# Penalties of one key tile: a product on VectorE in place of two matmuls on TensorE, last batch of a decoder layer

## The reference

```python
penalties = res * scope                          # 512 x 512 for a batch, one for all heads
log_pen = jnp.log(jnp.maximum(penalties, 1e-32))
scores = jnp.einsum('bhqd,bhkd->bhqk', q, k) / np.sqrt(HEAD_DIM)
scores = scores + log_pen[:, None, :, :]
probs = jax.nn.softmax(scores, axis=-1)
ctx = jnp.einsum('bhqk,bhkd->bhqd', probs, v)
x = _layernorm(x + ctx.transpose(0, 2, 1, 3).reshape(b, s, h))
```

## Time and profile before

| | us |
|---|---|
| median of 3 runs | 752.32 |
| the profiled execution | 752.63 |
| its span | 750.8 |
| TensorE busy (matmul) | 662.1 (88%) |
| VectorE busy | 593.8 (79%) |
| ScalarE busy | 475.9 (63%) |
| GpSimd busy | 324.7 (43%) |
| L1585, low half of the logarithm, 128 matmuls | 49.2 |
| L748, GpSimd's products, 128 | 167.3 |
| L1037, row maxima of self groups, 256 | 168.1 |

### The profile page before, as it was taken

How to read it: one execution, slowest core, us unless ns; L and a number is a source line. 1 busy time by engine, 2 the same in 40 slices (tenths; PEclk the granted TensorE clock), 3 DMA queues, 4 the chain that set the end, 5 groups by cost and what they waited for, 6 DMA issues and landing times.

```text
span 750.8 us, 10494 instructions
## 1 busy us (share of the span) xinstructions
PE 662.1 (88%) x3398; PEld 267.2 (36%) x3402; DVE 593.8 (79%) x1290; ACT 475.9 (63%) x795; POOL 324.7 (43%) x418
## 2 busy tenths in 40 slices
PE   6468989999899989999799999898898899987973
PEld 3233324443233243344232433342223235233441
DVE  3997988687898986678997867568997796836997
ACT  3515756646558868655469688454677776792965
POOL 6305868555665414646464126546722200101404
PEclk9678999989999999999999999999999999999997
DMA  2722352300322314312203403431511420000003
GB/s 92 205 62 85 109 149 95 105 8 21 108 74 83 92 46 115 87 46 73 71 26 87 109 24 87 109 91 24 157 48 43 130 68 22 3 4 1 1 1 112
DMA packets 35926, 53.98 MB, mean 72 GB/s; under 512 B 5281, under 2 KB 26913, under 8 KB 35873
## 3 DMA queue, kind: packets, MB, share of 16 engines
q1 hardware_dynamic: 35872, 53.31, 25.7%
HBM read 37.04 MB, written 14.68 MB: 69 GB/s over the span
## 4 chain that ended last, share of the span: by engine, by line
PE 52%; DVE 26%; POOL 8%; ACT 6%; issue 6%; DMA 2%; SPq 0%; POOLq 0%; DVEq 0%; ACTq 0%
PE ps L1604 11%; PE ps L1557 9%; PE ps L1580 9%; PE ps L1441 6%; DVE dist L1040 5%; PE ps L1544 5%; POOL probs L748 5%; ACT probs L933 4%; PE ps L1537 3%; DVE mx L1037 3%; PE ps L1584 2%; PE ps L1585 2%; DVE pen_a L1107 1%; DVE x L1077 1%; DVE stats L1062 1%
## 5 line engine op out<-in xcount | busy, mean ns | idle before, releaser
L1557 PE MATMUL ps<-KS,QS 96*128 96x512 bf16 x512 | 200.2, 394 | 37.8 <-DVE mx L1037 16.5
L933 ACT ACTIVATE probs<-ps 128x512 f32<-128x512 f32 x256 | 149.5, 596 | 120.5 <-PE ps L1580 66.1
L748 POOL TENSOR_TENSOR probs<-probs,penT 128x512 f32<-128x512 f32 x128 | 167.3, 1327 | 110.0 <-ACT probs L933 109.9
L1580 PE MATMUL ps<-QS,KS 108*128 108x512 bf16 x512 | 195.8, 384 | 10.7 <-ACT probs L933 5.6
L933 ACT ACTIVATE probs<-ps,mask_col 128x512 f32<-128x512 f32 x256 | 166.9, 688 | 45.7 <-PE ps L1580 43.4
L1037 DVE TENSOR_REDUCE mx<-ps 128x1 f32<-128x512 f32 x256 | 168.1, 682 | 34.7 <-PE ps L1557 34.1
L1040 DVE CUSTOM_DVE_ANT_0 dist<-ps,mask_rest 128x512 bf16<-128x512 f32 x192 | 125.7, 684 | 21.3 <-PE ps L1557 21.0
L1557 PEld LDWEIGHTS ps<-KS,QS 96*128 96x128 bf16 x512 | 50.7, 99 | 176.1 <-DVE mx L1040 61.9
L1580 PEld LDWEIGHTS ps<-QS,KS 108*128 108x128 bf16 x512 | 50.0, 98 | 87.9 <-ACT probs L933 49.5
L1604 PE MATMUL ps<-probs,v_s 128*32 128x512 f32 x512 | 69.1, 611 | 2.7 <-POOL probs L748 2.7
L1604 PE MATMUL ps<-probs,v_c 128*32 128x512 f32 x512 | 68.2, 604 | 0.9 <-ACT probs L933 0.9
(11 more groups left out here) (195 smaller groups left out, 937.0 us busy)
## 6 DMA issues: line engine op xcount, KB each, us to landing
parts_qs<-parts SPq DMA_DIRECT2D x8, 384.0 KB, 2.4
parts_ks<-parts SPq DMA_DIRECT2D x8, 384.0 KB, 2.8
KS<-parts_ks SPq DMA_DIRECT2D x16, 192.0 KB, 3.4
QS<-parts_qs SPq DMA_DIRECT2D x16, 192.0 KB, 3.8
parts_kc<-parts SPq DMA_DIRECT2D x8, 384.0 KB, 2.8
KS<-parts_kc SPq DMA_DIRECT2D x16, 192.0 KB, 2.9
parts_qc<-parts SPq DMA_DIRECT2D x8, 384.0 KB, 2.9
QS<-parts_qc SPq DMA_DIRECT2D x16, 192.0 KB, 3.4
```

What stands on the lines that cost most here:

```text
L748: g.tensor_tensor(probs[:, T % NP, :], probs[:, T % NP, :], penT[:, MUL_KT.index(kt), :], ALU.mult)\
L933: s_.activation(probs[:, T % NP, :], ps[:, exp_bank(T), :], ACT.Exp, bias=bias)\
L1557: mm(ps[:, MAX_BANKS[(TG * n + i) % AHEAD], :], QS[0:SK, slot, j, t * P:(t + 1) * P], KS[0:SK, slot, j, :], start=True, stop=True).then_in ...
L1580: ins = mm(o, KS[0:SM, slot, j, kt * P:(kt + 1) * P], QS[0:SM, slot, j, :], start=True, stop=not logged)
```

## The change

A key tile (`VEC_KT` = 1) of the self groups from batch `VEC_FROM` = 3 on, which is the last batch, gets its penalties by a product on VectorE after the exponential. Its penalties are prepared as `penT` (a third plane), not as logarithm halves. TensorE issues one matmul in place of three for these 16 tiles, and `context` of that key tile waits for VectorE's products and is issued a slot later. VectorE's job "penalise" is in the slot of the exponential and runs three slots late, behind that slot's row maximum and ahead of the other late jobs. The functions `by_vector`, `by_vector_until` and `kept` are new; `logs` counts only the tiles that still have a logarithm.

```diff
--- before.py
+++ after.py
@@ -44,9 +44,10 @@
 SILUS = 4
 RING = 4
 MUL_KT = (0, 2)
+VEC_KT, VEC_FROM = 1, 3
 
 DVE_LAG, ACT_LAG, POOL_LAG = 2, 0, 1
-DVE_LATE = {"norm": 3, "v": 3, "wo": 3, "lpB": 3}
+DVE_LATE = {"norm": 3, "v": 3, "wo": 3, "lpB": 3, "penalise": 3}
 ACT_LATE = {"middle": 3}
 POOL_LATE = {"low": 5, "shift": 0}
 NP = 8
@@ -72,6 +73,11 @@
 def place(what, part):
 
     return PARTS - 1 - part if what == "k" else part
+
+
+def by_vector(b, kt):
+
+    return b >= VEC_FROM and kt == VEC_KT
 
 
 class Step:
@@ -154,6 +160,10 @@
             at = [(0, ("shift", s.shift)), (3, ("m", s.shift))] + list(at)
         if s.p2 is not None:
             at = [(10, ("last_context", s.p2)), (10, ("oT", s.p2)), (15, ("norm", s.p2))] + list(at)
+        for slot in range(TG):
+            e = s.exp_at(slot)
+            if e and groups[e[0]][0] == "s" and by_vector(groups[e[0]][1], e[1] // GH):
+                s.items[slot].append(("penalise", *e))
         for slot, job in at:
             s.items[slot].append(job)
         for lo, hi, task in tasks:
@@ -338,7 +348,7 @@
         lp = sb("lp", [P, NT, S], F32, att)
         lpT_hi = sb("lpT_hi", [P, NT - len(MUL_KT), S], F16, att)
         lpT_lo = sb("lpT_lo", [P, NT - len(MUL_KT), S], F16, att)
-        penT = sb("penT", [P, len(MUL_KT), S], F32, att)
+        penT = sb("penT", [P, len(MUL_KT) + 1, S], F32, att)
         V = {w: sb("v_" + w, [P, NT, NH, VC], F32, att) for w in "sc"}
         probs = sb("probs", [P, NP, S], F32, att)
         mx = sb("mx", [P, 2, NT, GH], F32, att)
@@ -391,6 +401,7 @@
         rest_made = sem("rest_made")
         middle_made = sem("middle_parts_made")
         pen_applied = sem("penalties_applied")
+        pen_by_vector = sem("penalties_applied_by_vector")
         gate_ready = sem("gate_weights_ready")
         max_scores = sem("scores_for_max")
         max_done = sem("max_done")
@@ -482,7 +493,15 @@
 
         def logs(b, kt):
 
-            return len(log_kt) * b + log_kt.index(kt) + 1
+            return [(i, k) for i in range(b + 1) for k in log_kt if not by_vector(i, k)].index((b, kt)) + 1
+
+        def by_vector_until(n):
+
+            return GH * sum(kind == "s" and by_vector(b, VEC_KT) for kind, b, _ in groups[:n + 1])
+
+        def kept(b, kt):
+
+            return MUL_KT.index(kt) if kt in MUL_KT else len(MUL_KT)
 
         def multiplied(n, kt):
 
@@ -882,10 +901,12 @@
 
                         if kt in MUL_KT:
                             act.wait_ge(pen_applied, multiplied(last_self(b - 1), kt))
-                        else:
+                        elif by_vector(b - 1, kt):
+                            act.wait_ge(pen_by_vector, by_vector_until(last_self(b - 1)))
+                        elif not by_vector(b, kt):
                             act.wait_ge(exp_scores, TG * last_self(b - 1) + GH * (kt + 1))
-                    if kt in MUL_KT:
-                        s_.activation(penT[:, MUL_KT.index(kt), :], bank(u), ACT.Copy, scale=2.0 ** LN_SHIFT)\
+                    if kt in MUL_KT or by_vector(b, kt):
+                        s_.activation(penT[:, kept(b, kt), :], bank(u), ACT.Copy, scale=2.0 ** LN_SHIFT)\
                             .then_inc(side_free[u % 2], 1)
                     else:
                         s_.activation(lpT_hi[:, log_kt.index(kt), :], bank(u), ACT.Copy).then_inc(lp_hi_made, 1)
@@ -1092,7 +1113,7 @@
                     if b:
 
                         dve.wait_ge(lp_made, b)
-                        used(dve, *[unit[("lpB", b - 1, kt)] for kt in MUL_KT])
+                        used(dve, *[unit[("lpB", b - 1, kt)] for kt in range(NT) if kt in MUL_KT or by_vector(b - 1, kt)])
                 if k == 0:
                     leave(v.tensor_scalar(pen_a[:, :], z_row[:, :], -1.0, wi, ALU.mult, ALU.add))
                 elif k == 1:
@@ -1176,6 +1197,15 @@
                     penalty(*job[1:])
                 elif what == "norm":
                     normalise(job[1])
+                elif what == "penalise":
+                    n, i = job[1:]
+                    T, b = TG * n + i, groups[n][1]
+                    if groups[n][2] == 0 and i % GH == 0:
+
+                        used(dve, unit[("lpB", b, VEC_KT)])
+                    dve.wait_ge(exp_done, T + 1)
+                    v.tensor_tensor(probs[:, T % NP, :], probs[:, T % NP, :], penT[:, len(MUL_KT), :], ALU.mult)\
+                        .then_inc(pen_by_vector, 1)
                 elif what == "v":
                     w, b, i = job[1:]
                     full(dve, u)
@@ -1463,7 +1493,7 @@
                         ins.then_inc(side_full[u % 2], 1)
                 elif what == "lpB":
                     b, kt = job[1:]
-                    src = pen if kt in MUL_KT else lp
+                    src = pen if kt in MUL_KT or by_vector(b, kt) else lp
                     pe.wait_ge(pen_made if kt in MUL_KT else lp_made, b + 1)
                     turn(u, [src[:, t, kt * P:(kt + 1) * P] for t in range(NT)])
                 elif what == "x1T":
@@ -1566,7 +1596,7 @@
                     pe.wait_ge(shift_loaded, 16 * (n + 1))
                     if n < RING:
                         pe.wait_ge(own_rows_made, n + 1)
-                logged = kind == "s" and kt not in MUL_KT
+                logged = kind == "s" and kt not in MUL_KT and not by_vector(b, kt)
                 if logged and g == 0 and j == 0:
 
                     used(pe, unit[("lpB", b, kt)])
@@ -1598,6 +1628,8 @@
                 T = TG * n + GH * kt
                 if kind == "s" and kt in MUL_KT:
                     pe.wait_ge(pen_applied, multiplied(n, kt))
+                elif kind == "s" and by_vector(b, kt):
+                    pe.wait_ge(pen_by_vector, by_vector_until(n))
                 else:
                     pe.wait_ge(exp_done, T + GH)
                 for j in range(GH):
@@ -1621,7 +1653,8 @@
                     if e:
                         exp_tile(*e)
                         kt = e[1] // GH - 1
-                        by_product = groups[e[0]][0] == "s" and kt in MUL_KT
+                        kind, b, _ = groups[e[0]]
+                        by_product = kind == "s" and (kt in MUL_KT or by_vector(b, kt))
                         if kt >= 0 and e[1] % GH == (GH - 1 if by_product else GH - 2):
                             context(e[0], kt)
                     for job in s.items[i]:
```

## The result

The changed kernel took 760.16 us in the median (758.12 to 761.29, four runs), the kernel before 751.7 beside it: a ratio of 1.0095, 95% interval 1.0062 to 1.0128. The forecast was 755.3 in a range of 748.0 to 760.5. So it is slower, by 7 to 8 us where the sum said 3.0. It lies inside the range by 0.3 us, in the part that was left open for the rivals; the forecast's own range ended at 758.3. The rival that gave 760.3, the clock, was the nearest.

What follows compares the result with a forecast made beforehand. TensorE held 52% of the chain, VectorE 26%; VectorE was the fuller engine in groups three and four. Terms 0.7 - 0.9 + 1.8 + 1.8 - 0.4 = +3.0 us gave 755.3 us against the median, range 748.0 to 760.5.

Steps and rivals of the forecast that it cites:

- the forecast's own range: 753.3 to 758.3 us, for VectorE's queue and the meetings taking TensorE's gain and more, +1 to +6 us; chance 0.54.
- the clock: Rival: longer TensorE idling before 513.66 and 535.66 brings a second 1.2 GHz stretch, plus more meetings; +8 us, 760.3; chance 0.15.
- Removed: 32 matmuls off TensorE in the last batch's four self groups, 7.0 us, taken as the bound on any gain there.
- Preparation: One tile turned from pen, VectorE's low-half subtraction of 0.69 us dropped where VectorE idles anyway; taken as 0.
- First group: To the mark at 476.21: no TensorE gain, two meetings delay GpSimd; +0.7 us, bounds 0 and +1.5.
- meetings: VectorE's two-SBUF-input products and GpSimd instructions holding each other up: up to 1.1 us for VectorE, 0.4 for GpSimd each.
- Second group: TensorE's slot 3 comes 1.9 us sooner, a context product of 1.0 us moves behind it; -0.9 us, bounds -1.7 and +0.4.
- Third group: VectorE's queue from 512.92 to 527.30 takes four products, less 0.64 us idle; +1.8 us, bounds +0.7 and +3.5.
- Fourth group: Slot 3's maximum comes 3.0 us later, less 1.2 lead, and the moved context product adds 1.0; +1.8 us, bounds +0.3 and +3.
- Give-back: At 555.65, where VectorE waits 1.40 us for TensorE, part of the delay is returned; -0.4 us, bounds 0 and -1.4.
- Faster: Rival: TensorE's gain in slots 12 to 15 holds where TensorE is the bound; -5.0 us, 747.3; chance 0.21.
- Nothing: Rival: the delays are absorbed by 555 us and the first two group terms cancel; 752.5 us; chance 0.10.

Runs made afterwards that it cites:

- e3: Changed kernel without VectorE's products or any wait for them, key tile 1's penalties left out in the last batch: 754.78 us, ratio 1.0027.
- e9: Changed kernel with ten filler matmuls into a free bank ahead of TensorE's wait for GpSimd in the first group: 759.68 us, ratio 1.0104.
- e12: The changed kernel run once more without any edit, for its trace: 757.88 us, a single execution.
- e1: Changed kernel with the normalisation ahead of VectorE's product in slot 15, nothing else: 756.36 us, ratio 1.0061.
- e2: Changed kernel with VectorE's 16 products replaced by memsets of the same tile, those penalties left out in the last batch: 756.67 us, ratio 1.0067.
- e7: Key tile 3 in place of 1, its logarithm matmuls removed, no products, its penalties left out: 750.18 us, ratio 0.9960 against the kernel before.
- e6: Changed kernel with key tile 3 in place of 1 given to VectorE: 759.22 us, ratio 1.0083.
- e8: Kernel before the change with eight filler matmuls ahead of its third wait, the 2.73 us at 513.66: 752.74 us, ratio 1.0006.
- e4: Changed kernel with two filler score matmuls put back ahead of each of the 16 exponential tiles, products kept: 756.35 us, ratio 1.0066.
- e5: Changed kernel with both the normalisation ahead of VectorE's product in slot 15 and two filler matmuls a slot: 759.61 us, ratio 1.0086.
- e11: Changed kernel without products, those penalties left out, and with two filler matmuls in each of the 16 slots: 752.82 us, ratio 1.0002.

## Why the prediction was right or wrong

**Removed, 7.0 us: the size was right, the use was not.** It was taken as a bound, and the waits behind it took all of it, as e3 shows (1.0027 with nothing in their place).

**Preparation, 0.** Between the marks of 439.27 and 457.89 after and before differ by 0.01 us. Right.

**First group, +0.7.** The meetings were right. GpSimd's instructions at 466.71 and 468.28 took 1.61 and 1.71 us where unmet ones took 1.16 and 1.27: 0.45 a meeting, 0.4 predicted. By the Trainium skill (SBUF — State Buffer, Who interferes with whom) the two exclude each other for the whole instruction, which by the 0.61 us of an unmet product would be 0.6, an estimate; the trace has GpSimd lose less, and VectorE 0.54 at 466.09. Nine of the sixteen products took over 1 us, where a third was expected. e9 gives +0.82 for the step with the wait filled. What failed is the sentence that the wait would be about 2 us and cost no more than its length: it was 3.11, and in after's trace 1.40 us of lower clock came behind it.

**Second group, -0.9: the term that failed most.** The prediction followed VectorE to the maximum that slot 3 asks for, and took the normalisation as one piece of that queue. It did not ask who waits for the normalisation: TensorE, for the side bank, ahead of slot 3. That wait of 2.33 us and the clock behind it make +2.9 (+2.7 in e12). With the normalisation ahead (e1) +0.3 is left, and without meetings (e2) 0.0; the full -0.9 appears only without the products (e3).

**Third group, +1.8, measured +0.5 to the mark of 522.44, +1.4 to the matmul that the term was given for (e12: +0.7).** VectorE's part of it was 0.4: from the maximum of 512.92 to that of 526.69 it was 13.77 us before, and 530.79 - 516.59 = 14.20 after: +0.43 in place of +1.8. The reason is the one that the lower bound named. The rounding of the gate weights got out of GpSimd's way: 0.35, 0.29 and 0.29 us at 529.87 to 530.58, where the first three took 0.52, 1.25 and 1.13. That is 2.0 us, more than the 1.1 that the bound allowed for it. TensorE's matmul behind it came 1.1 us after the maximum was done and not 0.2, so VectorE's queue did not pace it there. The mechanism was named; its size was off.

**Fourth group, +1.8, measured +1.1 from mark to mark (e12: +1.6)**; in after a wait of 1.54 us for ScalarE and a fall at 541.34 are in it. **Give-back, -0.4:** none. VectorE waited 1.38 us at 561.03 as it had 1.40 before, but the marks did not come forward; a fall of the clock at 572.13, which e12 has not, adds 1.54.

**The rivals.** "Faster" is refuted by e3, e7 and e6: without products key tile 1 gains nothing, and key tile 3 gains 3.3 us that its products turn into a loss. "Nothing" fell with the timing. "The clock", at a chance of 0.15, gave the size nearest, and falls make 5.2 of the 8.3 us of after's trace. That it made the size is not shown: e2 and e3 have as much low clock (0.94 and 0.93) at +3.9 and +3.4, e9 without the first fall is no faster, and by the timed runs some 5 us come with the products. Its places were named wrongly too: it expected the third and fourth stall, and looked at the wait of 1.00 us before 476.21, which left the clock alone, as evidence against. The first and second group had the longer new waits. The terms of queue and meetings, taken from after less the falls (1.40 in the first, 3.38 - 1.99 = 1.4 in the second, 1.94 - 1.06 = 0.9 in the fourth, 1.54 at 572), leave about 3 us. That this is the sum's size is luck, for its parts are others: the third and fourth term, which gave the forecast its sign, measured 1.5 us in place of 3.6, and the two groups that were to cancel made 5.1.

**What stays open.** Each of the waits of 2.2 us and more between 457 and 600 us had a fall at it or just behind, 21 waits in 14 traces. Of the shorter ones some had one and some had not, with equal waits: 2.01 us in e8 and 2.01 in e4, or the pair of 1.01 and 0.74 us in after and in e12. What decides it was not found. It is a part of why e5 and e9 are no faster than the change, and of why single traces differ by 2 us. Whether the second group's loss is more wait or more clock was split only by e1 (both go together).

## What to carry to other kernels

Work taken off an engine that next waits for another engine buys a longer wait, and on TensorE a longer wait can cost more than its length (e9): price the wait that ends last in each stage, and name the chance of a lower clock behind each wait that grows. Where work is added to an in-order queue, list every instruction that shares its slot and ask who waits for each, the buffers handed back included. To split such a change, run all four corners: with and without the added work, each with the removed work gone and put back as idle work. The products' price was clear of noise in both columns here, where one trace's sum of falls pointed elsewhere.

## What the runs showed of the hardware

- More matmuls can cost no time: e3 to e11 adds 32 and goes from 1.0027 to 1.0002 (the intervals overlap a little); the ten of e9 take 1.40 us off a step of after's trace and 0.58 off e12's.
- After waits of 1.5 to 3.8 us, and at 572 us after two of 1.01 and 0.74 close together, TensorE was at 1.2 GHz (eight context matmuls 1.94 us against 1.06); behind the shorter of them in some executions and not in all. A fall cost 1.4 us of the path in the first step and 1.5 at 572 us; the same granted clock of 0.94 from 456 to 600 us went with sums of 3.9 (e2) and 8.3 us (after).
- A VectorE product of 128x512 f32 from two SBUF tiles took 0.67 to 1.52 us, 1.03 in the median; a memset of that shape took 485 ns each time.
